# Loading the experts' gathered token rows through a transposing DMA

## The reference, cut to what matters

```python
logits = x @ router_w
top_logits, top_indices = jax.lax.top_k(logits, 2)
scores = softmax(top_logits)
permuted = x[sorted_pos // 2]            # rows in order of their expert
for e in range(8):
    g, u = split(permuted * mask_e @ w1[e])
    out += where(mask_e, (silu(g) * u) @ w2[e], 0)
combined = (unpermuted out * scores).sum
shared = (silu(x @ w_gate) * (x @ w_up)) @ w_down
return x + combined + shared
```

## Time and profile before

| what | us |
|---|---|
| median of 3 runs | 952.84 |
| lowest, highest run | 952.15, 953.67 |
| the profiled execution, its own time | 953.63 |
| its span in the trace | 951.9 |

### The profile page before, as it was taken

How to read it: one execution, slowest core, us unless ns; L and a number is a source line. 1 busy time by engine, 2 the same in 40 slices (tenths; PEclk the granted TensorE clock), 3 DMA queues, 4 the chain that set the end, 5 groups by cost and what they waited for, 6 DMA issues and landing times.

```text
span 951.9 us, 23136 instructions
## 1 busy us (share of the span) xinstructions
PE 913.4 (96%) x8264; PEld 620.1 (65%) x8264; DVE 778.6 (82%) x1574; ACT 703.1 (74%) x1258; POOL 491.2 (52%) x495
## 2 busy tenths in 40 slices
PE   5588999999999999999999999999999999999996
PEld 3375667677677677677677677666655666666664
DVE  6789999999999999999999999987998754444443
ACT  6998888888888888888788888864656545555553
POOL 5336767566576575576675666521056513333333
PEclk9999999999999999999999999999999999999999
DMA  9934201010011001001001100314458713333323
GB/s 214 331 95 76 60 23 56 24 52 23 29 32 43 30 29 46 29 29 46 29 29 38 38 30 28 113 51 130 143 181 254 250 37 52 62 63 54 48 29 34
DMA packets 36750, 70.45 MB, mean 74 GB/s; under 512 B 3616, under 2 KB 24736, under 8 KB 36512
## 3 DMA queue, kind: packets, MB, share of 16 engines
q1 hardware_dynamic: 27184, 54.39, 18.0%
q0 software_dynamic: 9456, 14.59, 9.1%
HBM read 55.52 MB, written 18.68 MB: 78 GB/s over the span
## 4 chain that ended last, share of the span: by engine, by line
PE 79%; DVE 10%; ACT 4%; issue 3%; POOL 3%; DMA 1%; POOLq 0%; DVEq 0%; ACTq 0%
PE b_pj L350 23%; PE b_tr L369 9%; PE b_o L410 7%; PE b_sc L381 6%; PE b_pj L1366 5%; PE b_acc L453 5%; PE b_o L1401 5%; PE b_o L1493 3%; PE b_tr L1366 3%; PE b_sc L1366 3%; PE b_pt L400 3%; PE b_pj L1446 2%; PE b_pt L1390 2%; PE b_sc L1446 1%; PE b_tr L1446 1%
## 5 line engine op out<-in xcount | busy, mean ns | idle before, releaser
L725 POOL TENSOR_TENSOR rstd<-vareps,neghalf 128x4 f32<-128x4 f32 (+1 forms) x128 | 173.2, 1353 | 10.7
L718 POOL TENSOR_SCALAR vareps<-ssq,unit 128x4 f32<-128x4 f32 (+1 forms) x128 | 66.5, 519 | 210.3 <-DVE ssq L539 210.1
L350 PE MATMUL b_pj<-w_hi,xq 128*128 128x512 f16 x384 | 147.7, 385 | 1.1 <-DVE xq L707 0.9
L350 PE MATMUL b_pj<-w_lo,xq 128*128 128x512 f16 x384 | 147.1, 383 | 0.0
L465 ACT ACTIVATE sq<-b_pj 128x512 f32<-128x512 f32 x192 | 115.6, 602 | 32.7 <-PE b_pj L350 31.2
L539 DVE TENSOR_REDUCE ssq<-sq 128x4 f32<-128x512 f32 x192 | 130.3, 678 | 10.2 <-ACT sq L465 9.0
L1342 POOL DMA_INDIRECT out<-xn x39 | 60.8, 1558 | 135.6 <-ACT xn L1572 109.6
L369 PE MATMUL b_tr<-ident,nrm 128*128 128x128 f32 x768 | 120.4, 280 | 9.1 <-DVE nrm L550 4.6
L478 ACT ACTIVATE raw<-b_pj 128x512 f32<-128x512 f32 x192 | 117.2, 610 | 0.0
L369 PEld LDWEIGHTS b_tr<-ident,nrm 128*128 128x128 f32 x768 | 88.0, 141 | 44.0 <-DVE nrm L550 13.3
L550 DVE TENSOR_TENSOR nrm<-raw,rstd 128x512 f32<-128x512 f32 x128 | 107.9, 843 | 0.4
(11 more groups left out here) (329 smaller groups left out, 2218.3 us busy)
## 6 DMA issues: line engine op xcount, KB each, us to landing
nst<-in_ffw SPq DMA_DIRECT2D x40, 512.0 KB, 3.3
wload<-in_ffw SPq DMA_DIRECT2D x20, 512.0 KB
xbuf<-zero SPq DMA_DIRECT2D x13, 387.0 KB, 9.8
xn<-xbuf SPq DMA_DIRECT2D x9, 516.0 KB, 3.7
x_sb<-in_x SPq DMA_DIRECT2D x4, 512.0 KB, 13.3
wproj<-in_ctxT SPq DMA_DIRECT2D x1, 2048.0 KB, 10.2
xhl<-in_w_all SPq DMA_DIRECT2D x4, 512.0 KB, 17.0
wproj<-in_wprojT POOLq DMA_DIRECT2D x4, 512.0 KB, 5.8
```

The costliest lines, as they stand in the source:

```text
L350: last = pe.matmul(o, x, w[kind][:, k, at:at + BANK], start=(k == 0 and n_ == 0), stop=(k == KT - 1 and n_ == len(terms) - 1))
L725: pool.tensor_tensor(rstd[:, r % 2, c, :], vareps[:, r % 2, c, :], neghalf[:, 0:1].unsqueeze(2).to_broadcast(shape), ALU.pow)\
```

## The change

SP loads each group of four tiles by a transposing DMA into one of the three `stage` buffers, now named `gT`: 128 partitions, 4 blocks (two of the high part, two of the low), 512 rows. A second DMA brings only the 8 bytes at the end of each row into `xn`, with its own semaphore `xm_in`. The first transposing DMA waits until the stage buffers are free, the fourth and later ones until `first` of the group three before is done (`eh_done`). `gather_T`, `high_x`, the copy in `low_x` and the buffers `gh` and `gl` are gone; `first` takes its stationary side straight from `gT`.

```diff
+            gT = [w[:, :].bitcast(F16).rearrange("p (m r) -> p m r", r=TURN * P) for w in stage]
+
+            def turned(t, m):
+                return gT[t // TURN % len(gT)][:, m, t % TURN * P:(t % TURN + 1) * P]
...
-                    sp.dma_start(xn[:, a % NT:a % NT + b - a, :].bitcast(U32), x_rows[:, a:b, :]).then_inc(s[f"xg_in{q % 4}"], 16)
+                    if q == 0:
+                        sp.wait_ge(s["wl_done"], NPC)
+                    if q >= len(gT):
+                        sp.wait_ge(s["eh_done"], TURN * (q - len(gT)) + TURN)
+                    sp.dma_start_transpose(gT[q % len(gT)][:, :, 0:(b - a) * P], xbuf16[a * P:b * P, 0:2 * H])\
+                        .then_inc(s[f"xg_in{q % 4}"], 16)
+                    sp.dma_start(xn[:, a % NT:a % NT + b - a, 2 * H:ROW].bitcast(U32), x_rows[:, a:b, H:ROW // 2])\
+                        .then_inc(s[f"xm_in{q % 4}"], 16)
...
-                def gather_T(t):
+                def first(t, e):
+                    n = t % 2
                     if t % TURN == 0:
                         pe.wait_ge(s[f"xg_in{t // TURN % 4}"], 16 * (t // NT + 1))
-                    after(pe, "gl_done", t)
-                    for k in range(2 * KT):
-                        last = pe.transpose(b_x[:, k * P:(k + 1) * P], xrow(t)[:, k * P:(k + 1) * P], ident16[:, :])
-                    last.then_inc(s["gT_done"], 1)
...
-                        for m, (xx, w) in enumerate(((gh, w1h), (gh, w1l), (gl, w1h))):
+                        for m, (part, w) in enumerate(((0, w1h), (0, w1l), (KT, w1h))):
                             for c, o in enumerate((b_g[n], b_u[n])):
                                 at = k * 2 * F + c * F
-                                last = pe.matmul(o[:, :], xx[n][:, k * P:(k + 1) * P],
+                                last = pe.matmul(o[:, :], turned(t, part + k),
...
-                def high_x(t):
-                    n = t % 2
-                    act.wait_ge(s["gT_done"], t + 1)
-                    after(act, "eh_done", t - 1)
-                    act.activation(gh[n][:, :], b_x[:, 0:H], ACT.Copy).then_inc(s["gh_done"], 1)
...
                 def low_x(t):
-                    n = t % 2
-                    dve.wait_ge(s["gh_done"], t + 1)
-                    dve.tensor_copy(gl[n][:, :], b_x[:, H:2 * H]).then_inc(s["gl_done"], 1)
+                    if t % TURN == 0:
+                        dve.wait_ge(s[f"xm_in{t // TURN % 4}"], 16 * (t // NT + 1))
                     dve.tensor_tensor(uys[:, t:t + 1], uy[:, t:t + 1],
                                       xrow(t)[:, 2 * H + 2:ROW].bitcast(F32), ALU.mult)
```

More of the change, by code:

```diff
@@ L97, in build @@
         x_rows = xbuf.rearrange("(t p) d -> p t d", p=P)
+        xbuf16 = xbuf.bitcast(F16)
         n3 = zero[:, 0, 0:2 * H].bitcast(F32)
@@ L138, in build @@
                  "eah_done units_done unit_step x_out counts_read ctx_2048 pos_done wjob_done "
-                 "wsq_done wtot_done nst_in wst_in2 x ln_step mv_done rstd_done x_in0 x_in1 x_in2 x_in3 n3_pool rw16_done row_out rows_in codes_set steps_set eg_done xg_in0 xg_in1 xg_in2 xg_in3").split()
+                 "wsq_done wtot_done nst_in wst_in2 x ln_step mv_done rstd_done x_in0 x_in1 x_in2 x_in3 n3_pool rw16_done row_out rows_in codes_set steps_set eg_done xg_in0 xg_in1 xg_in2 xg_in3 xm_in0 xm_in1 xm_in2 xm_in3").split()
         s = {n: sem(n) for n in names}
@@ L1206, in build @@
             b_g, b_u, b_y = (b_pj[0], b_tr), (b_pj[1], b_sc), b_o
-            gh = [sb(f"gh{n}", [P, KT * P], F16, ph) for n in range(2)]
-            gl = [sb(f"gl{n}", [P, KT * P], F16, ph) for n in range(2)]
+            gT = [w[:, :].bitcast(F16).rearrange("p (m r) -> p m r", r=TURN * P) for w in stage]
+            def turned(t, m):
+                return gT[t // TURN % len(gT)][:, m, t % TURN * P:(t % TURN + 1) * P]
             uys = sb("uys", [P, ET], F32, ph)
@@ L1211, in build @@
             b_a = b_pt[:, :].bitcast(F16).rearrange("p (m c) -> p m c", m=2)
-            b_x = b_acc[:, :].bitcast(F16)[:, 0:2 * H]
             b_ey = [b[:, 0:H] for b in b_o]
@@ L1347, in _ @@
             def _(pe):
-                def gather_T(t):
+                def first(t, e):
+                    n = t % 2
                     if t % TURN == 0:
                         pe.wait_ge(s[f"xg_in{t // TURN % 4}"], 16 * (t // NT + 1))
-                    after(pe, "gl_done", t)
-                    for k in range(2 * KT):
-                        last = pe.transpose(b_x[:, k * P:(k + 1) * P], xrow(t)[:, k * P:(k + 1) * P], ident16[:, :])
-                    last.then_inc(s["gT_done"], 1)
-                def first(t, e):
-                    n = t % 2
-                    pe.wait_ge(s["gl_done"], t + 1)
                     if t < 2:
@@ L1417, in expert @@
                     return bass.RuntimeValue.of_register_unchecked(reg, min_val=0, max_val=E - 1)
-                def gather(t):
-                    return lambda: gather_T(t)
                 es = []
@@ L1425, in begin @@
                     es.extend((expert(0), expert(1), expert(2)))
-                    gather_T(1)
                     first(0, es[0])
                 def begin_end():
-                    gather_T(2)
                     first(1, es[1])
@@ L1524, in _ @@
                     (6, "up"): last_routes, (10, "up"): ranks, (20, "up"): load_codes,
-                    (31, "up"): gather(0), (31, "down"): begin, (32, "down"): begin_end,
+                    (31, "down"): begin, (32, "down"): begin_end,
                 })
@@ L1529, in _ @@
                     first(t + 2, es[t + 2])
-                    gather_T(t + 3)
                     es.append(expert(t + 3))
@@ L1576, in begin @@
                     act.wait_ge(s["units_done"], 1)
-                    high_x(1)
                     gate_x(0)
                     split(0)
-                    high_x(2)
                     gate_x(1)
@@ L1623, in _ @@
                 run_slots3(act, [(0, gate, "gate"), (0, weights, "weights"), (0, high, "high")],
-                           {(8, "gate"): gap_exp, (31, "gate"): lambda: high_x(0)})
+                           {(8, "gate"): gap_exp})
                 begin()
@@ L1627, in _ @@
                     gate_x(t + 2)
-                    high_x(t + 3)
                     split(t + 2)
```

1 line of the change is left out of this document (removed).

## The result

The changed kernel takes 943.37 us (median of four runs, 942.35 to 943.6), the kernel before, on the same chip, 952.74 us. The ratio is 0.9896, with a 95% interval of 0.9882 to 0.991. The forecast of 944.4 stands for a ratio of 0.9911: the direction and the place of the gain came out as forecast, and the gain is larger by about one microsecond.

The account below looks back on a forecast made before the run. TensorE was taken to bound the kernel; 38 tiles x 0.22 = 8.4 us of transposes came off 952.84, copies, loads and moved store costing nothing, giving 944.4 us. The range was 942.9 to 955.0, leaving out rival 2.

Parts of the forecast that it names:

- What bounds the kernel: Expert phase: TensorE is full from 790 to 930 us at 4.61 us a tile; no engine takes over at 4.39.
- What is removed from TensorE: Expert loop: four transposes a tile, 0.22 us, fully on the path for 38 tiles, 8.4 us off.
- What is removed elsewhere: Expert loop: ScalarE's copy of 377 ns and VectorE's of 281 ns per tile go, worth nothing by itself.
- What is added and where it is hidden: Group loads on DMA: ten transposing and ten row-end DMAs; up to 8.4 us costs nothing at the start, 17.6 later.
- T: Time from a group's issue until both its DMAs land, also the pace when queued; taken between 4 and 8 us.
- What is moved: Shared part's last store goes behind group 3; POOL starts near 786, some 10 us late, catches up, costing nothing.
- Rival 1: Phase start: load late there only, T between 8.4 and 14, time 944.4 to 950.0 us; chance 0.10.
- Rival 2: Group loads: transposing DMA becomes the bound, also through the moved store; slower from T = 14.6, 984.6 us at 19.6; chance 0.15.
- Rival 4: Output scatters: POOL never catches up after the late store, up to 10 us more, about 954.8 us; chance 0.02.
- rival 3: Expert loop: transposes stood in a shadow, such as the sequencer's register work, so no gain, 952.8 us; chance 0.02.

Follow-up runs that it names:

- The run with four loads: Changed kernel with each group's transposing DMA preceded by three further ones of the same rows into spare buffers; 948.96 us, ratio 0.9954 against the kernel before.
- the one with two: Changed kernel with each group's transposing DMA preceded by one further one of the same rows into a spare buffer; 942.47 us, ratio 0.9887 against the kernel before.
- seven loads: Changed kernel with each group's transposing DMA preceded by six further ones of the same rows into spare buffers; 993.61 us, ratio 1.0425 against the kernel before.
- the version with the products by DMA: Changed kernel with product_T's transposes also moved to DMA, their evictions gone, second three tiles behind first; 929.58 us, ratio 0.9744 against the kernel before.

## Why the prediction was right and wrong

**What bounds the kernel** held: TensorE did in both kernels, and no other engine took over, but for the wait for `low_T` at tile 0. **What is removed from TensorE** held in size: 8.4 us forecast, 8.0 measured with the transposes put back. Its reason held only because the copies went too, as told below.

**What is removed elsewhere** is the step that failed. It said: "Both engines wait for TensorE in the loop, so this is worth nothing by itself." That is true of ScalarE's copy (943.16 with it back). It is false of VectorE's: with it back the time is 952.5, with it gone from the kernel before 951.63. That VectorE waits for TensorE shows only that it has time over; at the moment TensorE asked for the copy, it was the last thing to arrive. Hence the mis-sized term: I gave the copies 0, and put the 0.04 us a tile that I had seen in `first` at the lower end of the range. It was 34 x 0.04 = 1.4 us by the chain of before (tiles 4 to 37), and 1.7 to 1.8 by the two runs that measure it. With it the sum is 952.84 - 8.4 - 1.4 = 943.0, beside 943.37 and 942.84 measured.

The same step hid a larger error of reasoning. "They lie on the path in full, since nothing ran beside them that TensorE waited for": something did, the ring over the copy at 4.61 us. By this ring the transposes alone, with VectorE's copy kept, would have gained nothing, as the run with that copy shows. That the forecast came out close is luck in this respect: the change removes both. The reader of the earlier trace rows could see it: the same 12 matmuls were 2.63 us in the loop and 2.59 at tile 0, where no copy was late.

**What is added and where it is hidden** held. T was taken as 4 to 8 us; the transposing DMA landed in 4.2 to 6.4 with 4.8 as the median, and the rows' ends in less than 6.05. The cover was somewhat less than the 8.4 I gave: the issue came 1.2 us later, since I had not read when the stage buffers come free, and `first` of tile 0 started at 762.63. That leaves 7.2 us to `first`. The run with four loads lies beyond that cover and pays the difference, the one with two doesn't. T was also meant as the pace of several in a queue; that pace is shorter than the landing, 2.2 and 2.8 us from one group's issue to the next at the start (755.39, 757.63, 760.39).

The estimate of T = 20.9 us from the Trainium skill, "VectorE: DVE Perf Modes", section "The three transpose paths", did not hold here: 16 blocks landed in 4.2 to 6.4 us. That the blocks go one after another was my assumption for it. The Trainium skill's "Advanced Engine Details and Errata", section "X-Bar Transpose (TRN2)", which calls transposing DMAs as fast as ordinary ones, is near: 4.8 us beside 3.7 for the plain load.

**What is moved** held: POOL's start was forecast near 786 and was 784.41, it caught up, and moving the store forward changed nothing.

**The rivals.** Rival 1 has its run (four loads, T = 4.69 + 6.25 = 10.9 us from the first issue): right in mechanism, but it left out that TensorE restarts at a lower clock. Rival 2 came true at seven loads. The late store was priced well (865.43 for 867); the pace of the loads after it was not, about 20.9 us a group for 17.4. Rival 4 did not happen. Neither did rival 3, but it was nearer than its 0.02: the transposes did stand in a shadow, that of the ring over VectorE's copy and not of register work, and with that copy kept its 952.8 is what was measured (952.5).

## What to carry to other kernels

At the engine that bounds the kernel, look for what arrives last before each of its steps, also where the wait is a few hundredths of a microsecond: a ring through other engines may stand just behind it, and then work taken from the bounding engine is worth only as much as the ring allows. A group of identical instructions that the chain prices differently at two places at the same clock (2.63 and 2.59 us) can be such a wait, as it was here. Here, with TensorE the bound and the DMA engines used to a third, transposes went well to a DMA that is issued ahead; measure the room by issuing the load several times.

## What the runs showed of the hardware

- After 3.8 us without work TensorE took 4.22 us for the 12 matmuls of `first` in place of 2.59 (four loads). In the run with four loads the first two matmuls take 0.83 us to the next two (767.02 to 767.85), the last ones 0.43 (770.21 to 770.64). Each has 512 columns, so these are the levels of 1.2 and 2.4 GHz (512 columns in 0.415 and in 0.215 us). The granted clock of 763 to 790, a mean over both, is 0.94, and from 790 on it is 1.00. With seven loads the same 12 take 5.07 us after 10.68 us without work (774.01), and 4.07 us after 4.00 us (931.03). The last place is different: there the first four still go at 0.43 to 0.44 us for two (931.03, 931.47, 931.90), and the lower level comes after them, while TensorE works (933.18 to 934.04: 0.86 us for two).

```profile
767.02 1.03 PE L1376 MATMUL b_pj<-w1h,wload 128*128 x2 [3.81 <-DMA wload<-xbuf]
767.85 1.06 PE L1376 MATMUL b_pj<-w1l,wload 128*128 x2
...
770.21 0.59 PE L1376 MATMUL b_pj<-w1l,wload 128*128 x2
770.64 0.59 PE L1376 MATMUL b_pj<-w1h,wload 128*128 x2
```

- A transposing DMA is dear for the queue that issues it: 1.3 to 2.9 us of SP for 512 rows in the changed kernel, and up to 4.8 us with four and seven loads a group (1.24 us in the median for the 128 rows of a tile in the version with the products by DMA, where the source is in SBUF). Four plain loads took 2.21 us together. With four in a row SP issued them without a pause (755.95, 757.40, 760.05, 762.20), at 1.4 to 2.6 us each.
- The load's packets are small. From the changed kernel to the one with each load twice the profile's page counts 20288 packets and 5.11 MB more, some 250 bytes each (77324 and 75.54 MB there), and each further load of every group adds the same (117900 packets with four, 178764 with seven). The kernel before has 36750 packets for 70.45 MB, the changed kernel:

```profile
DMA packets 57036, 70.43 MB, mean 75 GB/s; under 512 B 28896, under 2 KB 45024, under 8 KB 56800
```

- Beside dense traffic of transposing DMAs accumulating scatters landed later: in up to 7.7 us with seven loads, and in 3.80 us at the end of the same run, when the loads were over. Why they are stretched, by the DMA engines' time or in HBM, was not separated.
